# A four-layer image model on one core: the first attention's values kept by image row, the last attention's loads issued in pieces

## The reference, cut to what matters

```python
# layer 0: neighbourhood attention with 16 register keys
q, k, v = qkv[0], qkv[1], qkv[2]                    # (n, nh, s, e), s = 48*48
k_cat = concatenate([k, reg_k]); v_cat = concatenate([v, reg_v])
mask = make_neighbourhood_mask(7, 7, 48, 48)        # a 7 x 7 window, moved inward at the image's edge
scores = where(mask_cat, einsum('bnqe,bnke->bnqk', q, k_cat) * scale, NEG_INF)
o = einsum('bnqk,bnke->bnqe', softmax(scores), v_cat)
...
# layer 3: full attention, with relative positions by row and by column added to the scores
```

## Time and profile before

| | us |
|---|---|
| median of 3 runs | 4881.64 (4876.91 to 4882.69) |
| the profiled execution, its own time | 4893.03 |
| its span | 4891.2 |
| TensorE (PE) busy, sum over the span | 3500.2 |
| VectorE busy | 3579.1 |
| ScalarE busy | 2699.6 |
| GpSimd busy | 1499.8 |

### The profile page before, as it was taken

The page is one execution under the profiler, slowest core; times in us unless marked ns, Lnnn a source line. Parts: engine busy times, 40 slices in busy tenths (PEclk is TensorE's granted clock), DMA queues, the critical chain, the costliest instruction groups (busy, mean ns, idle before and its releaser), DMA issues. The chain is left out here.

```text
span 4891.2 us, 120325 instructions
## 1 busy us (share of the span) xinstructions
PE 3500.2 (72%) x47313; PEld 1818.4 (37%) x47313; DVE 3579.1 (73%) x3605; ACT 2699.6 (55%) x4416; POOL 1499.8 (31%) x907
## 2 busy tenths in 40 slices
PE   4487855317777766306877765766999999999996
PEld 3266632102222222101222212462665665665563
DVE  4354524869999946687999974456888887888884
ACT  1155524845554532863555542152888888888883
POOL 0011100019999940007999980000000000000000
PEclk8688887558888877656888887856999999999998
DMA  3424321342222220233222221242111111111113
GB/s 87 98 45 69 60 48 34 103 117 60 68 67 60 66 71 15 73 118 83 69 61 65 69 57 39 90 126 65 51 50 50 50 50 50 50 50 50 50 50 87
DMA packets 184511, 320.24 MB, mean 65 GB/s; under 512 B 90011, under 2 KB 129123, under 8 KB 180368
## 3 DMA queue, kind: packets, MB, share of 16 engines
q1 hardware_dynamic: 183952, 312.42, 24.4%
HBM read 203.73 MB, written 108.02 MB: 64 GB/s over the span
## 5 line engine op out<-in xcount | busy, mean ns | idle before, releaser
L1953 DVE TENSOR_REDUCE l3a_mx<-l3a_mx 128x2 f32<-128x768 f32 x1362 | 1231.5, 952 | 287.3 <-PE l3a_mx L1857 282.2
L1929 ACT ACTIVATE l3a_p<-l3a_s 128x384 f32<-128x384 f32 x2592 | 1163.1, 490 | 239.6 <-PE l3a_s L1879 231.1
L1372 POOL TENSOR_TENSOR l_scan_sc<-l_scan_s,l_scan_repc 128x768 f32<-128x768 f32 x576 | 1026.7, 1809 | 5.9 <-DVE l_scan_s L1350 5.7
L1879 PE MATMUL l3a_s<-l3a_q,l3a_k 125*32 125x384 f16 x10368 | 877.6, 331 | 36.5 <-issue 36.1
L1309 ACT ACTIVATE l_scan_da<-l_scan_da,l_scan_a 128x768 f32<-128x768 f32 x576 | 504.0, 875 | 630.7 <-PE l_scan_da L1233 630.7
L1857 PE MATMUL l3a_mx<-l3a_k,l3a_q 124*32 124x384 f16 x10896 | 737.2, 338 | 52.2 <-issue 32.5
L1891 PE MATMUL l3a_o<-l3a_p,l3a_vh 128*32 128x288 f32 x6920 | 608.0, 413 | 20.6 <-ACT l3a_out L1919 18.7
L1233 PE MATMUL l_scan_dup<-l_scan_du,l_scan_pick 96*128 96x512 bf16 (+1 forms) x1152 | 347.4, 390 | 372.0 <-DMA l_scan_dt<-l_dtp 213.7
L1363 POOL TENSOR_TENSOR l_scan_bup<-l_scan_dus,l_scan_repb 128x768 f32<-128x768 f32 x192 | 347.3, 1809 | 654.1 <-DMA l_scan_repc<-l_bcp 654.1
L1823 POOL TENSOR_TENSOR l3a_norm<-l3a_out,l3a_spread 128x576 f32<-128x576 f32 x25 | 35.8, 1433 | 1460.8 <-DMA l3a_spread<-l_inverses 1460.8
L1350 DVE TENSOR_TENSOR_SCAN l_scan_s<-l_scan_da,l_scan_s,l_scan_bu 128x768 f32<-128x768 f32 x256 | 450.6, 1802 | 2.3 <-issue 2.3
(11 more groups left out here) (192 smaller groups left out, 4378.6 us busy)
## 6 DMA issues: line engine op xcount, KB each, us to landing
l3a_q<-l_qx SPq DMA_DIRECT2D x26, 1944.0 KB
l_scan_du<-l_dup SPq DMA_DIRECT2D x144, 144.0 KB, 2.9
l_scan_dt<-l_dtp SPq DMA_DIRECT2D x144, 144.0 KB, 3.4
l_scan_repb<-l_bcp SPq DMA_DIRECT2D x48, 384.0 KB
l_scan_repc<-l_bcp SPq DMA_DIRECT2D x48, 384.0 KB
l3a_q<-l_hx SPq DMA_DIRECT2D x26, 288.0 KB
l_dtp<-l_prep_high_t SPq DMA_DIRECT2D x16, 432.0 KB, 3.1
l_dup<-l_prep_high_u SPq DMA_DIRECT2D x16, 432.0 KB, 3.1
```

What stands on the lines that cost most here:

```text
L1372: pool.tensor_tensor(SC[:, st % NSC, :], S[:, n, :], REPC[k % 2][:], ALU.mult).then_inc(weighted, 1)
L1879: mm = pe.matmul(s_ps[g % NS_PS][32 * c:32 * c + 32, 0:SW], K[e % NB][:, keys], Q[e % NB][:, variant(kt * 128 // RG), at:at + SW], start=T ...
L1929: act.activation(P[:, k % NP, third * SW:(third + 1) * SW], s_ps[g % NS_PS][:, 0:SW], ACT.Exp)\
L1953: dve.tensor_reduce(MX[:, h % NB, qt, 2 * pair:2 * pair + 2], mx_ps[bank][:, :, 0:RG], AX_X, ALU.max)\
```

## The change

Values of layer 0 are no longer kept by patch but by image row: the tile `VC` has, for each of the 3 columns of patches, all 48 rows of the image at slot (row modulo 4). `load_columns` takes 12 DMAs for a group of 4 heads, each of 22 x 12 rows of 64 numbers. Since a patch's window now begins at slot `kr % 4`, the places of rows and registers in scores and values depend on the patch (`row_place`, `regs_place`). GpSimd makes each head's operand with 10 small operations in place of one copy. The constants' loads and the values' stores move into the block of `v_projection`; the stores of an image start when its 18 tiles are done. In l0a `load_pair` moves ahead of `normalise`, and `load_shift` ahead of `store_out`. In layer 3 the loads of a head are issued in six pieces, at units 0, 14, 22, 30, 46 and 56; the first two `values` of a half are issued together, three units later than the first was, and ScalarE takes a half out one unit earlier.

```diff
-def load_windows(sp, tile, v_dram, vr_dram, group, strips, sem):
-    ...
-            for slot in range(4):
-                n = (KH - slot + 3) // 4
-                rows = image[kr + slot:kr + slot + 4 * n - 3:4, kc:kc + KW, :]
-                sp.dma_start(tile[32 * slot:32 * slot + KW, p, 0:n, :], rows.rearrange("n w e -> w n e")).then_inc(sem, 16)
+def row_place(p, r):
+    kr = window_of(p)[1][0]
+    return (kr + r) % 4, (kr + r) // 4 - kr // 4
+def regs_place(p):
+    kr = window_of(p)[1][0]
+    return (0, 0) if kr % 4 else (KH % 4, KH // 4)
+def load_columns(sp, tile, v_dram, group, slots, sem):
+    image = v_dram[group, :, :].rearrange("(h w) e -> h w e", w=W)
+    for slot in slots:
+        for c in range(NPW):
+            kc = window_of(c)[1][1]
+            sp.dma_start(tile[32 * slot:32 * slot + KW, c, :, :],
+                         image[slot:H:4, kc:kc + KW, :].rearrange("n w e -> w n e")).then_inc(sem, 16)
@@ layer0_attention, SP
-                    windows(h + 1, [0])
-                    if h + 3 < NPAIR:
-                        load_pair(sp, h + 3)
-                    windows(h + 1, [1])
+                    columns(h + 1)
@@
                     if h >= 1:
+                        if h + 2 < NPAIR:
+                            sp.wait_ge(scored, h * IPH)
+                            load_pair(sp, h + 2)
                         normalise(h - 1)
-                    windows(h, [2])
+                    if h + 1 < NPAIR:
+                        load_shift(h + 1)
                     if h >= 1:
                         store_out(h - 1)
-                    if h + 1 < NPAIR:
-                        load_shift(h + 1)
@@ layer0_attention, GpSimd, copy_values
-                        pool.tensor_copy(VH[h % 2 * 2 + e][:, :, :, 0:HD], VW[g % 2][:, :, :, cols]).then_inc(v_copied, 1)
+                    for home, cols in heads:
+                        for blk in range(4):
+                            pool.tensor_copy(home[:, NPW:NPT - NPW, blk, :].rearrange("p (s c) e -> p c s e", c=NPW),
+                                             vc[:, :, 1 + blk:8 + blk:2, cols]).then_inc(v_copied, 1)
+                        pool.tensor_copy(home[:, 0:NPW, :, :], vc[:, :, 0:4, cols]).then_inc(v_copied, 1)
+                        pool.tensor_copy(home[:, NPT - NPW:NPT, :, :], vc[:, :, ROWS4 - 4:ROWS4, cols]).then_inc(v_copied, 1)
+                    pool.wait_ge(v_copied, 2 * h * COPIES + 12)
+                    for home, cols in heads:
+                        ... (4 operations on 32 partitions each: the registers' values in, two places cleared)
+                    pool.wait_ge(v_copied, 2 * (h + 1) * COPIES)
@@ layer3_attention
-    AHEAD, JOIN_AT, TURN_AT, INVERT_AT = 4 * CYC, 1, 3, 6 * CYC
+    AHEAD, JOIN_AT, TURN_AT, INVERT_AT = 4 * CYC, 1, 3, 32
+    QUERIES_AT, ROWS_AT = (14, 30, 46, 56), 22
@@ values_at
-            return [(e, x // THIRDS - 1) if x >= THIRDS else (e - 1, KPH - 1)]
+            e, k = (e, x // THIRDS - 1) if x >= THIRDS else (e - 1, KPH - 1)
+            return [] if k % KT == 0 else [(e, k - 1), (e, k)] if k % KT == 1 else [(e, k)]
@@ half_ends_at
-            e, x = divmod(g - THIRDS // 2 - 1, UPH)
+            e, x = divmod(g - 1, UPH)
@@ layer3_attention, SP
-                        load_head(sp, (i * HPB + e + 2) % BH, (e + 2) % NB)
-                        store_out(sp, i * HPB + e, i * HPB + (e + 1))
+                        load_keys(sp, later, buf)
+                        queries(0)                                # waits for scored = unit 14
+                        sp.wait_ge(scored, i * ST + (e * UPH + ROWS_AT + LEAD))
+                        load_rows(sp, later, buf)
+                        queries(1)
+                        store_inverses(sp, i * HPB + e, i * HPB + (e + 1))
+                        queries(2)
+                        queries(3)
+                        store_out(sp, i * HPB + e, i * HPB + (e + 1))
```

More of the change, by code:

```diff
@@ L41 @@
 QROWS0 = 3 * HD + KH + KW
-REG_AT = (KH % 4, KH // 4)
+ROWS4 = H // 4
 VG = 4
@@ L363, in _ @@
                 sp.wait_ge(loaded, n_loads)
+                if behind_loads is not None:
+                    behind_loads(sp, done)
+            if fill is not None:
+                @block.gpsimd
+                def _(pool):
+                    fill(pool)
             @block.tensor
@@ L449, in layer0_attention @@
     KALL = QROWS0 + 1
+    COPIES = 10
     with Scope(nc, "l0a") as s:
         VH = [s.sb(f"vh{i}", [128, NPT, 4, VO]) for i in range(4)]
-        ones = s.sb("ones", [128, 4])
+        ones = s.sb("ones", [128, NPT, 4])
         P = s.sb("p", [128, NP, 4, PQ])
@@ L526, in load_shift, with columns @@
                       .then_inc(shift_loaded, 16)
-                def windows(h, strips):
+                def columns(h):
                     group, odd = (h + 3) // 2, (h + 1) % 2
                     if h >= 1 and group < VGROUPS:
-                        if strips[0] == 0 and not odd:
-                            sp.wait_ge(v_copied, 4 * (group - 1))
-                        load_windows(sp, VW[group % 2], v_dram, vr_dram, group, [3 * odd + x for x in strips], v_loaded[group % 2])
+                        if not odd:
+                            sp.wait_ge(v_copied, 4 * COPIES * (group - 1))
+                        load_columns(sp, VC[group % 2], v_dram, group, [2 * odd, 2 * odd + 1], v_loaded[group % 2])
                 def normalise(h):
@@ L651, in scores @@
                     q = Q[h % NB][:, e, p * PQ:(p + 1) * PQ]
-                    for r in range(KH):
-                        blk, slot = divmod(r, 4)
-                        at = (kr + r) * W + kc
-                        pe.matmul(out[32 * slot:32 * slot + KW, blk, :], k[:, e, at:at + KW], q, start=True, stop=True)
-                    slot, blk = REG_AT
-                    pe.matmul(out[32 * slot:32 * slot + NREG, blk, :], k[:, e, L:LK], q, start=True, stop=True)\
-                      .then_inc(scored, 1)
+                    places = [(*row_place(p, r), slice((kr + r) * W + kc, (kr + r) * W + kc + KW)) for r in range(KH)]
+                    places.append((*regs_place(p), slice(L, LK)))
+                    for slot, blk, keys in sorted(places, key=lambda x: (x[1], x[0])):
+                        n = keys.stop - keys.start
+                        mm = pe.matmul(out[32 * slot:32 * slot + n, blk, :], k[:, e, keys], q, start=True, stop=True)
+                    mm.then_inc(scored, 1)
                 def values(n):
@@ L664, in values @@
                     if n % QPH == 0:
-                        pe.wait_ge(v_copied, n // QPH * 2 + 2)
+                        pe.wait_ge(v_copied, (n // QPH + 1) * 2 * COPIES)
                     for blk in range(4):
@@ L1761, in store_sums, with store_inverses @@
               .then_inc(sums_loaded, 16)
-        def store_out(sp, row, count):
+        def store_inverses(sp, row, count):
             sp.wait_ge(inverted, count + LEAD)
@@ L1772, in store_out @@
                   .then_inc(inv_spread, 16)
+        def store_out(sp, row, count):
             sp.wait_ge(divided, count + LEAD)
@@ L1781, in _ @@
                 for h in range(2):
-                    load_head(sp, h, h)
+                    load_keys(sp, h, h)
+                    load_rows(sp, h, h)
+                    for v in range(VAR):
+                        load_queries(sp, h, h, v)
                 for i in range(NB):
@@ L2010, in build @@
             inv_dram = dram("l0_inverses", [BH // 2, 2 * L], F32)
-            VW = [s0.sb(f"vw{i}", [128, NPT, 4, VG * HD]) for i in range(2)]
+            VC = [s0.sb(f"vc{i}", [128, NPW, ROWS4, VG * HD]) for i in range(2)]
+            RV = s0.sb("rv", [128, NH // VG, VG * HD])
             Q = [s0.sb(f"queries{i}", [QROWS0 + 1, 2, L], F16) for i in range(3)]
@@ L2165, in shape_constants @@
     k["l0_qmask"], k["l0_places"] = out_of_reach, places
-    ones = np.zeros((128, 4), np.float32)
-    for r in range(KH):
-        ones[32 * (r % 4):32 * (r % 4) + KW, r // 4] = 1
-    ones[32 * REG_AT[0]:32 * REG_AT[0] + NREG, REG_AT[1]] = 1
+    ones = np.zeros((128, NPT, 4), np.float32)
+    for p in range(NPT):
+        for (slot, blk), n in [(row_place(p, r), KW) for r in range(KH)] + [(regs_place(p), NREG)]:
+            ones[32 * slot:32 * slot + n, p, blk] = 1
     k["l0_ones"] = ones
```

110 lines of the change are left out of this document (57 added, 53 removed).

## The result

The changed kernel takes 4724.7 us (median of 4 runs, 4716.2 to 4730.4), the kernel before 4879.3 beside it. The ratio is 0.968 (95% interval 0.9665 to 0.9698), 155 us less. The forecast was 4661 us, 221 us less.

What follows compares the result with a forecast made beforehand. Bounds: a late values' transfer, SP's issue of small DMAs in l0qk, an interrupted TensorE in l0a and l3a. -9 - 52 - 68 - 88 - 4 = -221 us, from 4881.6 to 4661 us; range 4620 to 4730, its own 4635 to 4690.

Steps and rivals of the forecast that it cites:

- l0qk, -52 forecast: l0qk: with fewer value loads in SP's queue, stores leave on time; -55 less 3 given back, between -55 and -40.
- The 3 us given back: l0qk: 3 us allowed for slots whose 870 KB are not away when their buffer is wanted.
- Values' stores, -9 forecast: Values' projection: half the stores move under it (about 8 us), one barrier goes (about 1); gain between nothing and 12.
- l0a, -68 forecast: l0a, nine pairs: 84.6 us lost, all but 1.9 us a pair regained; bounds -85 and -40.
- The waits for keys and for the maxima's row: l0a: TensorE's waits of 3.71 and 5.01 us, to go as `load_pair` and the maxima's row are issued earlier.
- I leave 1.9 us for each of nine pairs: l0a: half an "issue" wait and the slow clock after it stay, giving 28.3 us a pair.
- rival A: l0a: the 870 KB DMA burst still stops TensorE, 5 us a pair stay; 4700 us, chance 0.18.
- GpSimd, nothing forecast: l0a: 20 operations of 0.4 us, 8 us a pair from 2.3; TensorE's wait for `v_copied` costs nothing under some 23 us.
- Rival C: l0a: GpSimd becomes the bound and the kernel is slower than before, 4890 us or more; chance 0.02.
- l3a, -92 forecast: l3a: loads in pieces no longer stop TensorE, -88 (bounds -94 and -60); take-out order -4 (between -19 and +10).
- The three round starts: l3a: three loop round starts, 32.80 instead of 27.88 us for that half, about 15 us in all, stay.
- The rule against the pieces: l3a: quoted page's rule, given little; it would come out in rival B, l3a doesn't gain, 4749 us, chance 0.10.

Runs made afterwards that it cites:

- The split: Changed kernel with each of the six `l0_places` loads (37 rows) issued as two, of 32 and 5 rows: 4693.4 us, ratio 0.9608.
- three parts: Changed kernel with `load_pair` issued in three parts of 290 KB at units 0, 8 and 14: 4709.6 us; with `l0_places` loads also split, 4696.1 us.
- six parts: Changed kernel with `l0_places` loads split and `load_pair` in six parts of 144 KB at units 0, 3, 8, 13, 16, 19: 4679.0 us, ratio 0.9574.

## Why the prediction was right or wrong

The number lies in the range with some luck: the three parts of layer 0 fell outside their own bounds, one loss was not priced at all, and l0qk's gain made up for 6 us of it. The second and third paragraphs below hold the two steps that were wrong.

*l0qk, -52 forecast, -57.8 measured.* The step held as it stood: the stores leave on time, slots of 8.08 us. The 3 us given back were not needed: the two waits of before of 6.6 and 6.9 us for stores of queries are gone with the constants' loads. The other 2.8 us are at the stage's two ends (first stores 0.5 us sooner, last slot 0.5 shorter, `load_pair` 1.8 sooner behind the last store). One reading was slightly off, without effect: a value load of before has 66 or 88 rows, not 77 to 88.

*Values' stores, -9 forecast, +15.7 measured.* This is the step that failed, and it is 25 of the 58 us by which the profiled executions fall short of the forecast difference of 221. It said that the 12 constant loads "take 12 us and fit between the projection's start and its 18th tile", at the stretch's mean rate of 171 GB/s. The split shows that the rate of a load depends on its shape: with 37 rows, one engine's rate, 222 rows in 43.6 us, some 7 us for each load. With the split the stage ends at 80.3 us, 7.8 earlier than before, so the rest of the step was right to about 1 us; the barrier's "about 1 us" in it is shown by no row. The bounds stopped at a gain of nothing, since I gave this part no way to lose. What I should have read is the order: a load moved ahead of the stores is in front of them in the DMA queue too. The Trainium skill had the rule, in DMA: Bandwidth & Descriptors, section "Why a DMA increments its semaphore by 16 and not by 1": the number of engines is the largest up to 16 that divides the slowest dimension of both sides, and 127 partitions put everything on one. The trace agrees, with 6.5% of 16 engines busy for 37 rows. By that rule, as an estimate, the 36 rows of `l0_qmask` take 12 engines; no run here shows these loads alone.

*l0a, -68 forecast, -38.9 measured in the nine pairs, and +5.1 in pair 0.* The waits for keys and for the maxima's row went, as the steps said. Mis-sized was "I leave 1.9 us for each of nine pairs": the stop, with the slow clock behind it, takes 31.5 - 27.7 = 3.8 us of a pair (3.0 to 4.3 by the spread of the unchanged code), the 27.7 being a pair without the burst. That is rival A's mechanism, which I had priced at 5 us a pair. The floor was also too low: I took the first pair's 26.4 us, and even with hardly any pair's bytes it is 27.7. Together they make the 5.1 us a pair that are missing. The profile was to show a clock above 0.95; it is 0.91 over the stage. Pair 0's +5.1 is partly this execution: in three others of the same code pair 0 has no stop over 0.7 us and takes 25.6 to 28.4. One thing I had against rival A, that three pairs had the burst and no stop, was no evidence: TensorE was waiting for keys in those pairs at that time. The first of the moved steps, `load_pair` ahead of the sums, brought nothing measurable by itself. I haven't tried the maxima's row alone.

*GpSimd, nothing forecast.* Right, and the estimate of 0.4 us for a large copy (0.346 measured) and 0.3 to 0.5 for the small ones (0.13 to 0.38) did no harm. No engine waits for it. Rival C stayed far off.

*l3a, -92 forecast, -91.0 measured.* The mechanism held: cutting the loads took the stops away. In the order in which I added the parts up they are -81 for the pieces (1399.9 to 1319.1, with the split of the inverse sums in it) where I had -88, and -10 for the order of values and take-out where I had -4; both are in their bounds, and that the errors cancel to 1 us is luck. Taken the other way round the order is worth 29 and the pieces 62 (1371.1 to 1308.9), so there is no single share for either. Why what stays without the pieces is worth more where stops are was not settled: a stop's cost may depend on where it meets the loop of scores, and I have no run that moves one and not the other. Who stands instead was also another: not ScalarE, whose waits for scores fell from 148.9 to 139.9 us, but TensorE at VectorE's maxima, 11 us more. The three round starts stayed at some 5 us each, as forecast.

The rule against the pieces, in the Trainium skill, Runtime: NRT & Kernel Launch, section "Instruction fetch mechanics" (instructions stream in blocks and the cost is mostly hidden), is contradicted here: TensorE stops after 9 us with the DMA engines at 0.79 in l3a and after 5 us at 0.87 in l0a, and cutting the transfer takes the stop away. The same section says that a taken branch breaks the prefetch, and the stop at each round start agrees (3.31 us of "issue" in the profile of before, 32.85 against 27.75 us for that half in the one after).

## What to carry to other kernels

A transfer moved ahead of others needs its own shape read first: the loads of 37 rows went at one engine's rate, and what was issued behind them waited; in 32 rows and the rest they held nothing up. Where TensorE stands at "issue" a few us behind a large load, cut the load and space it by TensorE's own progress, and look at the stops that are left: three parts brought nothing that could be measured, six took the stage out of its spread. Before trusting a clean stretch as the floor, ask what it lacks besides the wait in question. And compare a stage by its own events: a fixed window of the span shifts against the stage when something ahead of it gets shorter.

## What the runs showed of the hardware that I had not expected

- Loads of 37 rows of 4640 bytes ran at 27 GB/s with 6.5% of 16 DMA engines busy, the work of one; in parts of 32 and 5 rows the same bytes held nothing up (a stage 23.4 us shorter).
- While data held the DMA engines at over 100% in l0a, no packet of instructions landed for 3.3 us, and TensorE stood for 3.53 us. With bursts of 870 KB the stops were up to 3.7 us over all runs, with 290 KB up to 3.7, with 144 KB up to 1.4.
- With a dozen stops of 0.7 to 1.4 us (six parts) the granted clock stayed at 1.00, the upper level, over the ten pairs; with stops of 2.1 to 3.5 us it was 0.91 over the same work, and 0.50 in the 4 us behind one of 3.53 us.
